# An attention and mixture-of-experts kernel on one core: five hand-set tables of the attention schedule changed

## What is computed

```python
q_f, k_f = taylor_exp(q), taylor_exp(k)              # [1, x/2, (x outer x)/(4*sqrt2)]
y1 = tril(q_f @ k_f.T) @ v                           # 512 x 512 per head and batch
y2 = (q_f @ k_enc_f.T) @ v_enc                       # first 128 tokens, other weights
z = 1.0 / ((q_f * (k_enc_f.sum() + cumsum(k_f))).sum(-1) + EPS)
x = layernorm(x + ((y1 + y2) * z) @ Wout.T)
top1, gate = router(x @ wr + br)
x = layernorm(x + gate * (gelu(x @ w1[top1] + b1[top1]) @ w2[top1] + b2[top1]))
```

## Time and profile before

| | us |
|---|---|
| median of 3 runs | 1216.52 |
| lowest, highest | 1216.51, 1217.79 |
| the profiled execution | 1213.65 |
| its span, first to last instruction | 1211.9 |
| granted TensorE clock, mean | 0.937 of full |

### The profile page before, as it was taken

The page is one execution under the profiler, slowest core; times in us unless marked ns, Lnnn a source line. Parts: engine busy times, 40 slices in busy tenths (PEclk is TensorE's granted clock), DMA queues, the critical chain, the costliest instruction groups (busy, mean ns, idle before and its releaser), DMA issues. The chain is left out here.

```text
span 1211.9 us, 16762 instructions
## 1 busy us (share of the span) xinstructions
PE 1080.4 (89%) x5296; PEld 629.2 (52%) x5297; DVE 690.0 (57%) x1050; ACT 427.4 (35%) x804; POOL 598.2 (49%) x571
## 2 busy tenths in 40 slices
PE   5799889989989989998998998983479999999994
PEld 4344355445445445544544544463356766677663
DVE  5597875684684686568468468546423334333342
ACT  2345433533433452453343343400023233332331
POOL 1477754654674565555465466510124454444442
PEclk9799999989989999998998998986589999999998
DMA  6635442443453254334244333014551100111010
GB/s 213 243 114 178 123 151 107 130 152 118 153 149 134 92 171 141 124 103 156 98 155 152 118 118 106 1 35 179 220 236 33 33 30 29 34 35 32 25 31 2
DMA packets 54110, 134.90 MB, mean 111 GB/s; under 512 B 5854, under 2 KB 10176, under 8 KB 51746
## 3 DMA queue, kind: packets, MB, share of 16 engines
q1 hardware_dynamic: 50306, 124.81, 30.3%
q0 software_dynamic: 3744, 9.31, 2.5%
HBM read 87.73 MB, written 47.29 MB: 111 GB/s over the span
## 5 line engine op out<-in xcount | busy, mean ns | idle before, releaser
L377 ACT ACTIVATE w<-slot 128x1024 f32<-128x1024 f32 (+1 forms) x256 | 234.8, 918 | 217.8 <-PE slot L714 217.2
L337 POOL TENSOR_TENSOR wsum<-w 128x1024 f32<-128x1024 f32 x64 | 163.6, 2556 | 242.0 <-DVE w L483 242.0
L732 PE MATMUL osum<-w,values 128*64 128x512 f32 (+3 forms) x1280 | 260.3, 502 | 17.7 <-ACT att L406 11.8
L480 DVE SCALAR_TENSOR_TENSOR w<-w,mask 128x256 f32<-128x256 f32 (+1 forms) x192 | 195.9, 1020 | 113.3 <-ACT w L377 112.8
L483 DVE TENSOR_SCALAR w<-w 128x1024 f32<-128x1024 f32 (+3 forms) x256 | 190.0, 748 | 45.0 <-ACT w L377 34.9
L340 POOL TENSOR_TENSOR wsum<-wsum,w 128x768 f32<-128x768 f32 x64 | 121.2, 1894 | 62.5 <-DVE w L483 62.0
L1196 PE MATMUL down<-w,active 128*128 x624 | 143.6, 384 | 2.5 <-ACT active L1142 2.5
L1208 PE MATMUL up<-w,rowsT 128*128 x312 | 142.6, 600 | 0.7 <-ACT rowsT L1131 0.7
L1142 ACT ACTIVATE active<-upT,b 128x128 f32<-128x128 f32 x312 | 84.9, 383 | 157.7 <-PE upT L1220 157.7
L714 PE MATMUL slot<-qop,kop 64*128 64x512 f32 (+3 forms) x640 | 127.8, 429 | 9.4 <-issue 8.1
L1196 PEld LDWEIGHTS down<-w,active 128*128 128x128 f32 x624 | 117.1, 193 | 18.5 <-issue 3.8
(11 more groups left out here) (185 smaller groups left out, 1185.3 us busy)
## 6 DMA issues: line engine op xcount, KB each, us to landing
kop<-k_rows SPq DMA_DIRECT2D x32, 640.0 KB, 4.7
qop<-q_rows SPq DMA_DIRECT2D x32, 512.0 KB, 5.8
w<-in_w SPq DMA_DIRECT2D x16, 1024.0 KB, 9.4
inv<-inv_rows SPq DMA_DIRECT2D x56, 256.0 KB, 5.7
k_rows<-kh SPq DMA_DIRECT2D x32, 320.0 KB
k_rows<-kl SPq DMA_DIRECT2D x32, 320.0 KB
q_rows<-qh SPq DMA_DIRECT2D x32, 256.0 KB
q_rows<-ql SPq DMA_DIRECT2D x32, 256.0 KB
```

Of the source, the lines that this page charges most:

```text
L337: pool.tensor_tensor(dst, src[:, :, 0:N], src[:, :, N:2 * N], ALU.add).then_inc(wsummed, 1)
L377: act.activation(w[:, n % 2, :, at:at + cols], slot[u % 2][:, :, 0:cols], ACT.Square, bias=HALF_ROOT).then_inc(squared, 1)
L480: dve.scalar_tensor_tensor(src[:, :, 0:cut], src[:, :, 0:cut], 0.5, mask[:, 0:cut].unsqueeze(1).to_broadcast([P, 2, cut]), ALU.add, ALU.mu ...
L732: last = pe.matmul(osum[n % 2][HD * s:HD * s + HD, q0:N], values[:, j, h * HD:h * HD + HD], w[:, n % 2, s, at:at + N - q0], start=(u == 0) ...
```

## The change

Only tables and one reading place differ. The sums are copied out at unit 0 of the next pair instead of its unit 3, the denominators are summed at unit 3 instead of unit 2, and the `att` ring has 14 slots instead of 12. Late value pieces stand in gaps 0 to 4, projections one gap earlier, output products at 18, 20, 22 and 24 with the early value pieces between them. Splitting x moves one gap forward; normalisation moves two gaps back, moments, deviation, centring and the turned rows one. The router moves to gap 31, so its result is read at the first gap of the batch after, and once behind the loop.

```diff
-RING, ATT, INV = 4, 12, 4
-V_LATE_AT = {0: 0, 2: 1, 4: 2, 5: 3, 6: 4}
-QK_AT = {10: 0, 12: 1, 14: 2, 16: 3, 18: 4}
-OUT_AT = {15: 0, 20: 1, 21: 2, 22: 3}
-V_EARLY_AT = {23: 0, 24: 1, 25: 2, 26: 3, 27: 4}
-TURN_AT, ROUTER_AT = {28: 0, 29: 1}, 30
-XH_GAP, XL_GAP = 7, 8
-INVERT_GAP, NORM_GAP, MOMENTS_GAP, CENTRE_GAP, RSTD_GAP = 1, 6, 24, 26, 25
-COPY_UNIT, DEN_UNIT = 3, 2
+RING, ATT, INV = 4, 14, 4
+V_LATE_AT = {0: 0, 1: 1, 2: 2, 3: 3, 4: 4}
+QK_AT = {9: 0, 11: 1, 13: 2, 15: 3, 17: 4}
+OUT_AT = {18: 0, 20: 1, 22: 2, 24: 3}
+V_EARLY_AT = {19: 0, 21: 1, 23: 2, 25: 3, 27: 4}
+TURN_AT, ROUTER_AT = {29: 0, 30: 1}, 31
+XH_GAP, XL_GAP = 6, 7
+INVERT_GAP, NORM_GAP, MOMENTS_GAP, CENTRE_GAP, RSTD_GAP = 1, 8, 25, 27, 26
+COPY_UNIT, DEN_UNIT = 0, 3
...
-                    if b > 0 and g - 1 == ROUTER_AT:
-                        logits_of(b - 1)
+                    if b > 1 and g == 0:
+                        logits_of(b - 2)
...
+            logits_of(B - 2)
```

## The result

| | before | after |
|---|---|---|
| median of the runs, us | 1216.5 | 1228.7 |
| lowest, highest | 1216.1, 1217.8 | 1223.9, 1233.3 |
| ratio, 95% interval | | 1.0096 (1.0075 to 1.0116) |
| profiled execution: span, mean clock | 1211.9, 0.937 | 1222.1, 0.939 |

The change costs 1%, 12 us. The direction was forecast, but 40 us were. The forecast's waits can be seen in the trace; most of its size is not there.

What follows compares the result with a forecast made beforehand. VectorE and GpSimd, as one serial path, were taken to bound stretches with few fillers. Batches 1 to 6 at +5.3 us each (32), batch 0 +2 and batch 7 +6 gave +40, median 1256.5 us, range 1222 to 1278.

Steps and rivals of the forecast that it cites:

- sums and denominators: Gaps 4 and 20: TensorE's waits for the copied sums go, 0.86 us a batch; denominators book nothing more.
- front stretch: Gaps 5 to 18: TensorE loses 10.4 us a batch to waits and slow clock against 7.8 before, +2.6 us.
- turned rows: Batch end: turned rows wait about 2.9 us for centred y, and their present 0.55 us wait goes.
- router: Batch end: the second turned half is copied late behind GpSimd's addition of gap 29, 1.2 us more (0 to 2).
- the path's length: VectorE's and GpSimd's steps in one row up to the last projection's low half: 34.0 us with the start.
- slow clock behind the last wait: First output product, behind the fifth projection's wait: TensorE at its lower clock, one slowdown of 1.7 us booked.
- The Trainium skill's count of slow stretches: Front waits: charging all three 1.7 us of half-rate clock would add 3.4 us a batch; the forecast rejected it.
- Batch 7: Last batch: turned rows +3 us, later normalisations 3 before the first output product; +6 us (1 to 10).
- Batch 0: First batch: first projection waits about 3 us for xl, of which +2 us (0 to 4) counted.
- A: Batch end hides its longer chain, so only 15 us remain: 1232 us; chance 0.13.
- B: GpSimd lets VectorE go first, so the front's waits go, 5.1 us a batch gained: 1182 us; chance 0.17.
- C: The front gains what the batch end costs, so the two cancel: 1216 us; chance 0.06.

Runs made afterwards that it cites:

- the second: The changed kernel run once more, with nothing altered: 1232.7 us, ratio 1.0141.
- The front tables by themselves: Kernel before with earlier copy, later denominators, larger ring, plus new value-piece, projection, normalisation, x-split and first-output-product places; batch end as before: 1207.9 us, ratio 0.9935.
- the run with the end tables: Kernel before with earlier copy, later denominators, larger ring, plus new places from output products to router; front as before: 1231.7 us, ratio 1.0117.
- the copy part alone: Kernel before with only the sums' copy at unit 0, denominators at unit 3 and the ring of 14: 1204.3 us, ratio 0.990.
- two further small edits: On kernel before with copy, denominators and ring changed: VectorE's small-loads wait put behind batch 0, router moved to gap 3 of the batch after next: 1192.1 us, ratio 0.978.

## Why the prediction was right in sign and wrong in size

Per batch, for batches 3 to 6 of the profiled execution:

| term | forecast | measured | how |
|---|---|---|---|
| sums and denominators | -0.9 | -0.9 | waits of gaps 4 and 20 gone (alone: -1.5) |
| front stretch | +2.6 | -0.7 | 7.1 lost instead of 7.8 |
| turned rows | +2.4 | +1.4 | 1.91 instead of 0.55 |
| router | +1.2 | 0 | no wait |
| sum | +5.3 | -0.2 | 98.9 against 99.1 |

The six batches 1 to 6 together were forecast at +32 us. They measured +2.1 in the first trace and +8.5 in the second, which has more slow stretches. The 30 us that the forecast had too much on the first trace's span are these six batches; batch 7, forecast too high, and batch 0 and the rest of the span, forecast too low, about cancel.

**The front stretch failed, by 3.3 us.** Its mechanism stood: TensorE waits for xl, for kl, for ql, in that order, and nothing there waits when GpSimd's additions are cut short. Two terms of its sum were too large. First, the path's length: 34.0 us with its start were forecast up to the low half that the last projection waits for; 470.05 - 437.68 = 32.4 were measured. I had added 0.1 us of handing over to each of GpSimd's eleven additions, 1.1 us, but the stretch by which I had tested the sum, 6.73 us against 6.51, held a hand-over already and was shorter than its sum without one; the other 0.5 us I can't name. The first projection, where the path was 10.4 us against a start of 448.12 - 437.68 = 10.44, came out exact; the excess lies in the longer piece behind. Second, I booked 1.7 us of slow clock behind the last wait, since the output product behind a wait of 1.41 us had taken 5.36 us. Behind 1.72 us it took 3.72, full clock. One row was read as a rule. The stretch at half clock came behind the first wait (449.1 to 452.5), inside the path's time, where it costs nothing. Together 3.3 us. The front tables by themselves fit this: 580.3 us for batches 1 to 6 against 582.7 without them.

The sum of the path also left something out without a reason: the low parts of q and k, 2.1 us of VectorE up to the start of the last projection. By its own rule of one serial path they belonged in it, and the forecast would have been further off. The rows of L472 above show why nothing was lost: they ran beside GpSimd. That this term could be left out was luck.

**The Trainium skill's count of slow stretches** (page "TensorE: Matmul & The Clock Gate", section "HAM oscillation — how this bites in real kernels"), by which each long wait would cost 1.7 us more, was further off than the sum: a usual batch had two slow stretches, not more than three. The page counts so for a kernel whose waits are 3 to 5 us each; of the three waits here only the first is as long. What my sum lacked, and the rule has, is that the number of stretches can grow: it goes with executions of one kernel that lie 9 us apart, and at the end of the batch it doubled in the run with the end tables.

**The end of the batch was right in its place, and 1.0 us too long.** The addends that failed are in these rows of GpSimd and VectorE, changed kernel, batch 3:

```profile
411.04 0.20 POOL L352 TENSOR_TENSOR rstd<-mv,y_eps 128x4 f32<-128x4 f32 x1
411.31 1.02 POOL L355 TENSOR_TENSOR rstd<-rstd,y_minus_half 128x4 f32<-128x4 f32 x1
412.30 1.26 POOL L347 TENSOR_TENSOR wsum<-wsum,w 128x512 f32<-128x512 f32 x1
```

```profile
412.37 2.32 DVE L532 TENSOR_SCALAR y<-y,mv,rstd 128x256 f32<-128x256 f32 x4 [1.95 <-POOL rstd L355]
```

From the start of gap 26 (405.42) the additions end after 5.6 us, as forecast (5.7). The deviation behind them took 1.3 us from start to start, not the 1.8 of the earlier trace rows, and the four centrings with GpSimd's addition 2.32, not the 2.79 of the sum: half a microsecond each. The router's 1.2 us came at one batch in this trace, at three in the next, and at all six, with 2 us, once the deviation stood earlier. So it is a chain just at its limit, as the bounds of 0 to 2 said. I took a value near the middle for what is either 0 or 1 and a slow stretch with it.

**Batch 7** was forecast at +6 and measured at -0.7 in this trace, +4.1 in the next. Its turned rows wait 6.03 us instead of 3.97, where 7 was forecast. Its first output product waits 2.41 us for a normalised pair instead of 0.82, where I had booked 3 more. The denominators ahead wait 1.2 us where they waited 3.2 before, which I had not set against it. **Batch 0** was forecast at +2, from a wait for xl of about 3 us, and came out at +5 with that wait at 4.51. In the next trace the load came 1.2 us later than in the kernel before, the wait for xl was 2.94, and the batch ended 2.7 us later, near the forecast. With the copy part alone it was 3.7. That VectorE's wait for the load holds up batch 0 is shown by the run that moves it; why the load lands at different times was not settled.

**The rivals.** A (1232: the end hides its chain, and 15 us remain) comes nearest in time, with 1228.7 and 1232.7 measured, but by luck and not by its reason: the end did cost, the front did not. B (GpSimd lets VectorE go first) is refuted by the waits for xl of 3.1 us. C (both sides cancel) comes near batches 1 to 6 of the first trace, not the median; what cancels in part is a copy part that gains 12 us and tables that cost 24 to 28 on top of it.

## What to carry to other kernels

Where two engines stretch over each other, add up the steps that do so as one queue (not those that run beside the other engine) and ask which filler's reader comes last on it; moving a step ahead on that queue only moves the wait. Of a gain and a loss in the same change, run each half alone: here an edit of three numbers was worth 1%, and with two further small edits 2%. Do not make a rule of a single slow row, and do not add a hand-over that the test of the sum already holds.

## What the runs showed that I had not expected

The same schedule took batches of 98.9 and of 103.1 us in one execution. The difference is one wait of 1.1 us at the router and two further stretches of 3.4 us at a granted clock of 0.50 to 0.53, TensorE's lower level of 1.2 GHz. Runs of the kernel before spread over 2 us in its first set and up to 7 later, runs of the changed kernel over 9.

GpSimd's step on 128 x 4 elements (L352) took 0.20 us with VectorE idle, and 0.66 in the earlier trace rows, where VectorE's masked step ran beside it. VectorE's busy time fell by 17 us of 63 a batch when GpSimd's additions were cut, with its own instructions unchanged. More than a quarter of a busy share can be standing. But a step with an operand in PSUM (L472) took 0.68 us beside an addition and without one.
